# Two causal attentions in one kernel: the first pair's row maxima sent in two halves, with its first eight score blocks taken between the maxima

## The reference

```python
s1 = jnp.einsum('bhtd,bhsd->bhts', q1, k1) * scale + mask
s2 = jnp.einsum('bhtd,bhsd->bhts', q2, k2) * scale + mask
a1 = jax.nn.softmax(s1, axis=-1)
a2 = jax.nn.softmax(s2, axis=-1)
out = jnp.einsum('bhts,bhsd->bhtd', a1 - lam * a2, v)
```

## Time and profile before

| what | value |
|---|---|
| time before, median of 3 runs | 866.46 us (866.29 to 870.01) |
| the profiled execution's own time | 866.14 us |
| its span, first to last instruction | 864.4 us |
| mean granted clock of PE | 0.928 of full speed |
| first attention, first max step to last value product | about 64 to 376 us |
| second attention, likewise | about 472 to 618 us |
| busy share of PE, DVE, ACT, POOL | 88%, 61%, 50%, 50% |

### The profile page before, as it was taken

The page is one execution under the profiler, slowest core; times in us unless marked ns, Lnnn a source line. Parts: engine busy times, 40 slices in busy tenths (PEclk is TensorE's granted clock), DMA queues, the critical chain, the costliest instruction groups (busy, mean ns, idle before and its releaser), DMA issues. The chain is left out here.

```text
span 864.4 us, 12823 instructions
## 1 busy us (share of the span) xinstructions
PE 757.0 (88%) x3664; PEld 366.7 (42%) x3664; DVE 523.5 (61%) x1345; ACT 431.6 (50%) x922; POOL 430.2 (50%) x751
## 2 busy tenths in 40 slices
PE   3938999999999999954984789999569999999995
PEld 2322222223222222212752223332148888888884
DVE  3649777777777777323553877785035555555555
ACT  1431566656666655742132166776524455455552
POOL 1751556664234323421222123334277999799994
PEclk9985999999999999985997699999869999999997
DMA  5393740110020011012049362433221222122121
GB/s 183 122 295 92 160 90 15 38 47 13 20 61 18 15 45 39 20 39 67 0 148 290 88 186 68 127 98 95 66 79 48 61 61 68 51 64 71 61 64 56
DMA packets 60076, 69.84 MB, mean 81 GB/s; under 512 B 14905, under 2 KB 40858, under 8 KB 60011
## 3 DMA queue, kind: packets, MB, share of 16 engines
q1 hardware_dynamic: 60016, 69.15, 28.4%
HBM read 47.35 MB, written 15.47 MB: 73 GB/s over the span
## 5 line engine op out<-in xcount | busy, mean ns | idle before, releaser
L696 ACT ACTIVATE top<-ps 128x512 f32<-128x512 f32 (+3 forms) x384 | 171.0, 490 | 133.4 <-PE ps L643 133.3
L643 PE MATMUL ps<-mid 99*128 99x512 bf16 (+3 forms) x576 | 184.1, 335 | 8.2 <-ACT mid L696 5.0
L626 PE MATMUL ps<-mid 96*128 96x512 bf16 (+3 forms) x512 | 173.2, 360 | 15.5 <-PEq L231 11.1
L738 DVE CUSTOM_DVE_ANT_0 ps<-ps,keep 128x512 f32<-128x512 f32 (+3 forms) x320 | 161.7, 529 | 27.4 <-PE ps L626 26.8
L1479 PE MATMUL ps<-xp,wp 128*128 128x512 f32 (+1 forms) x600 | 149.3, 399 | 16.6 <-ACT wp L1531 8.7
L663 PE MATMUL ps<-top,mid 128*33 128x512 f32 (+3 forms) x768 | 161.8, 500 | 0.0
L1479 PEld LDWEIGHTS ps<-xp,wp 128*128 128x128 f32 (+1 forms) x600 | 114.6, 192 | 42.5 <-ACT xp L1533 9.1
L643 PEld LDWEIGHTS ps<-mid 99*128 99x128 bf16 x576 | 53.9, 98 | 180.8 <-ACT top L696 102.9
L820 POOL TENSOR_SCALAR_AFFINE_SELECT top<-top 128x128 f32<-128x128 f32 x256 | 71.2, 291 | 110.5 <-ACT top L696 108.1
L696 ACT ACTIVATE mid<-ps 128x512 f32<-128x512 f32 (+1 forms) x192 | 82.1, 493 | 65.1 <-PE ps L643 42.4
L742 DVE TENSOR_REDUCE top<-ps 128x1 f32<-128x512 f32 x128 | 88.2, 689 | 36.5 <-PE ps L626 35.8
(11 more groups left out here) (204 smaller groups left out, 815.5 us busy)
## 6 DMA issues: line engine op xcount, KB each, us to landing
mid<-part_scratch SPq DMA_DIRECT2D x9, 1152.0 KB, 8.8
part_scratch<-top SPq DMA_DIRECT2D x18, 384.0 KB, 5.3
top<-in_w SPq DMA_DIRECT2D x16, 396.0 KB, 3.9
cw_s<-combine_rows SPq DMA_DIRECT2D x48, 128.0 KB, 3.0
part_scratch<-top SPq DMA_DIRECT2D x18, 256.0 KB, 5.2
mid<-part_scratch SPq DMA_DIRECT2D x9, 384.0 KB, 3.9
top<-inverse_scratch SPq DMA_DIRECT2D x12, 256.0 KB
top<-in_w SPq DMA_DIRECT2D x8, 384.0 KB, 5.1
```

Source lines behind the costliest of these rows:

```text
L626: nc.tensor.matmul(ps[:, s_bank(turn), 0:w], queries(pair, m)[0:PARTS, i * P:(i + 1) * P], keys(pair, m)[0:PARTS, c * 512:c * 512 + w], st ...
L643: nc.tensor.matmul(ps[:, ST_BANK + n % AHEAD, 0:w], keys(pair, m)[0:STACK, j * P:(j + 1) * P], queries(pair, m)[0:STACK, q0:q0 + w], start ...
L696: nc.scalar.activation(pr[:, n % RING, 0:w], ps[:, ST_BANK + n % AHEAD, 0:w], ACT.Exp, scale=0.25).then_inc(p_ready, 1)
L738: ins = nc.vector.tensor_tensor_reduce(bank, bank, msk[:, 512 - w:512], -1.0 if low else 1.0, 3e38 if low else -3e38, ALU.add, ALU.min if ...
```

## The change

In both attentions the maxima of pair 0 are sent in two halves. The order on PE becomes:

1. max steps 0 to 16; after step 10 the transpose of the first half (row groups 0 to 3 of both maps, which POOL has split once step 7 is reduced);
2. scores 0, 1, 2, which wait for the first half's rows;
3. blocks 0 to 7: at each a wait for its exponential, the score three further (none from block 5 on), and one max step (17 to 24); value products 0 to 5 in pairs at blocks 3, 5 and 7;
4. max steps 25 to 35, with value products 6 and 7 and the transpose of the full maxima after step 27;
5. scores 8, 9, 10, which wait for the second half's rows; then the old loop from block 8, which at blocks 8 to 13 takes 3, 3, 3, 3, 2, 2 max steps in place of one, so that from block 14 on it is where the old one was.

DVE does its steps in the same order; its quantisation pieces of blocks 1, 3, 5 and 7 of pair 0 now follow max step 35 one behind the other. The six-bank ring ends after turn 8. The parts lie in `mt` by map, and every pair's rows go in two transfers (one a map, three rows each) where there were three (one a part); pair 0 has two for each half. ACT waits, before its first exponential, for the writes to DRAM of the stage before, since the exponentials now begin earlier over the same memory.

```diff
+                HALF, HALF_AT, FIRST, CATCH = 8, 10, 17, (3, 3, 3, 3, 2, 2)
...
+                    if n == HALF_AT:
+                        maxima_turn["half"], turns = turns, turns + 1
...
+                HALF_TURN = sum(map(alone, range(HALF)))
+                BEFORE = HALF + len(CATCH) + LEAD - sum(CATCH)
+
+                def behind(n):
+
+                    if HALF <= n < HALF + len(CATCH):
+                        done = BEFORE + sum(CATCH[0:n - HALF])
+                        return range(done, done + CATCH[n - HALF])
+                    return (n + LEAD,) if HALF <= n < BLOCKS - LEAD else ()
 
                 def s_ring(turn):
-                    return S_RING + AHEAD if turn < PAIR else S_RING
+                    return S_RING + AHEAD if turn < HALF else S_RING
...
 # TensorE
-                            if n % PAIR == 0:
-                                pe.wait_ge(landed, 48 * (pair + 1))
+                            if n == 0:
+                                pe.wait_ge(landed, 32)
+                            if n == HALF or (n % PAIR == 0 and pair > 0):
+                                pe.wait_ge(landed, 32 * (pair + 2))
...
-                        for n in range(LEAD):
+                        for n in range(FIRST):
+                            max_step(n)
+                            if n == HALF_AT:
+                                maxima("half")
+                        for n in range(AHEAD):
+                            score_step(n)
+                        for n in range(HALF):
+                            pe.wait_ge(p_ready, n + 1)
+                            if n + AHEAD < HALF:
+                                score_step(n + AHEAD)
+                            max_step(FIRST + n)
+                            if n in (3, 5, 7):
+                                value_step(n - 3)
+                                value_step(n - 2)
+                        for n in range(FIRST + HALF, BEFORE):
                             max_step(n)
                             if n == PAIR + 3:
+                                value_step(HALF - 2)
+                                value_step(HALF - 1)
                                 maxima(0)
-                        for n in range(AHEAD):
+                        for n in range(HALF, HALF + AHEAD):
                             score_step(n)
-                        for n in range(BLOCKS):
+                        for n in range(HALF, BLOCKS):
...
-                            if n + LEAD < BLOCKS:
-                                max_step(n + LEAD)
-                            if k in GROUP_AT and n > LAG:
+                            for later in behind(n):
+                                max_step(later)
+                            if k in GROUP_AT and n > HALF + LAG:
...
 # ScalarE
+                        if first:
+                            for u in range(len(UN) - SLOTS, len(UN)):
+                                act.wait_ge(*unit_written(0, u))
...
 # VectorE
-                        for n in range(LEAD):
+                        for n in range(BEFORE):
                             max_step(n)
+                            if n == HALF_AT:
+                                maxima("half")
                             if n == PAIR + 3:
                                 maxima(0)
...
-                            if n + LEAD < BLOCKS:
-                                max_step(n + LEAD)
+                            for later in behind(n):
+                                max_step(later)
...
 # GpSimd
+                            of = slice(0, NT) if half is None else slice(4 * half, 4 * half + 4)
+                            done = 3 * (pair + 1 if half != 0 else 0)
+                            if half == 0:
+                                pool.wait_ge(s_maxed, HALF_TURN)
...
-                        split(0)
+                        split(0, 0)
                         for n in range(BLOCKS):
...
+                            if n == HALF:
+                                split(0, 1)
...
 # SyncE
-                        def rows(pair):
-
-                            sp.wait_ge(s_maxed, maxima_turn[pair] + 1)
-                            for j in range(3):
-                                sp.dma_start(stack[PARTS + j:PARTS + j + 1, 2 * pair:2 * pair + 2, :]
-                                             .rearrange("o m t -> o (m t)"),
-                                             mrow[16 * j:16 * j + 16, :]).then_inc(landed, 16)
+                        def rows(pair, half=None):
+
+                            sp.wait_ge(s_maxed, maxima_turn["half" if half == 0 else pair] + 1)
+                            for m in range(2):
+                                to, at, n = stack[PARTS:STACK, 2 * pair + m, :], 24 * m, 24
+                                if half is not None:
+                                    to, at, n = to[:, 512 * half:512 * (half + 1)], 24 * half + 12 * m, 12
+                                sp.dma_start(to, mrow[at:at + n, :]).then_inc(landed, 16)
...
                         def ahead(pair):
-                            rows(pair)
+                            rows(pair, 1 if pair == 0 else None)
...
+                        rows(0, 0)
                         ahead(0)
```

More of the change, by code:

```diff
@@ L527, in attention, with part @@
                 mx = sb(f"mx{layer}", [P, 2, 4, 2], F32, here)
[L528 removed]
+                mr = sb(f"mr{layer}", [P, 2, NT], F32, here)
                 mt = sb(f"mt{layer}", [P, P], BF16, here)
[L530 removed]
+                zero = sb(f"zero{layer}", [P, 2, NT], F32, here)
                 mrow = sb(f"mrow{layer}", [48, P], BF16, here)
[L533 to L534 removed]
+                def part(j, half):
+                    if half is None:
+                        return mt[:, 0:48].rearrange("p (m j i) -> p m j i", m=2, j=3)[:, :, j, :]
+                    return mt[:, 24 * half:24 * half + 24].rearrange("p (m j i) -> p m j i", m=2, j=3)[:, :, j, :]
                 if first:
@@ L632, in maxima @@
                             turn = maxima_turn[pair]
-                            pe.wait_ge(mt_ready, pair + 1)
-                            pe.wait_ge(s_maxed, turn - S_RING + 1)
+                            if pair == "half":
+                                pe.wait_ge(mt_ready, 1)
+                            else:
+                                pe.wait_ge(mt_ready, pair + 2)
+                            pe.wait_ge(s_maxed, turn - s_ring(turn) + 1)
                             nc.tensor.transpose(psb[:, s_bank(turn), 0:P], mt[:, :], idb[:, :]).then_inc(s_ready, 1)
@@ L725, in max_step @@
                             if k == 0 and pair >= 2:
-                                dve.wait_ge(mt_ready, pair - 1)
+                                dve.wait_ge(mt_ready, pair)
                             dve.wait_ge(s_ready, turn + 1)
@@ L751, in maxima @@
                             dve.wait_ge(s_ready, turn + 1)
-                            if pair > 0:
-                                dve.wait_ge(landed, 48 * pair)
+                            if pair == 0:
+                                dve.wait_ge(landed, 32)
+                            elif pair != "half":
+                                dve.wait_ge(landed, 32 * (pair + 1))
                             nc.vector.tensor_copy(mrow[:, :], psb[0:48, s_bank(turn), 0:P]).then_inc(s_maxed, 1)
@@ L798, in _ @@
                         nc.gpsimd.memset(mt[:, :], 0.0).then_inc(cleared, 1)
-                        nc.gpsimd.memset(zero[:, :], 0.0).then_inc(cleared, 1)
+                        nc.gpsimd.memset(zero[:, :, :], 0.0).then_inc(cleared, 1)
                         pool.wait_ge(cleared, 2)
[L802 to L813, removed]
-                            nc.gpsimd.tensor_tensor(part(2), mr[:, 0, :], part(1), ALU.subtract).then_inc(mt_ready, 1)
@@ new lines, in split @@
+                        def split(pair, half=None):
+                            of = slice(0, NT) if half is None else slice(4 * half, 4 * half + 4)
+                            done = 3 * (pair + 1 if half != 0 else 0)
+                            if half == 0:
+                                pool.wait_ge(s_maxed, HALF_TURN)
+                            else:
+                                pool.wait_ge(nm_ready, pair + 1)
+                                pool.wait_ge(s_ready, maxima_turn[pair - 1 if pair > 0 else "half"] + 1)
+                            a, rest, nil = nm[:, pair % 2, :, of], mr[:, :, of], zero[:, :, of]
+                            to = [part(j, half) for j in range(3)]
+                            nc.gpsimd.tensor_tensor(to[0], a, nil, ALU.add).then_inc(pch, 1)
+                            pool.wait_ge(pch, done + 1)
+                            nc.gpsimd.tensor_tensor(rest, a, to[0], ALU.subtract).then_inc(pch, 1)
+                            pool.wait_ge(pch, done + 2)
+                            nc.gpsimd.tensor_tensor(to[1], rest, nil, ALU.add).then_inc(pch, 1)
```

(3 more changed lines are left out.)

4 lines of the change are left out of this document (2 added, 2 removed).

## The result

The changed kernel takes 869.47 us (median of 20 runs, 867.5 to 873.7) against 867.69 for the kernel before in 20 runs beside it; the ratio is 1.0028, 95% interval 1.0014 to 1.0041, which is 2.4 us slower (1.2 to 3.6). The forecast was 866.4, no change against the median of 866.46 it started from, with a range of 863.0 to 870.0: the time lies in the range, but a slowdown clear of noise was not forecast. The kernel before has 1.2 us more in these 20 runs than in the three behind the forecast, so the ratio says more than the two absolute times. Its profiled execution took 869.56 us with a span of 867.6, against 866.14 and 864.4.

The account below looks back on a forecast made before the run. A chain of DVE reductions bounds the fronts, PE the loop after them. 866.14 + 0.5 + 0.7 + 0.4 - 1.6 = 866.1 us (fronts, low clock, rows), plus a third for the median: forecast 866.4, range 863.0 to 870.0.

Parts of the forecast that it names:

- the accounting of VectorE's waits in the fronts: Both attentions' fronts (first max step to the shared point): waits put into DVE make them 0.5 and 0.7 us later.
- the shared point: Transpose of pair 1's maxima at block 13, where both orders meet; forecast 96.4 and 502.5 us, before 95.89 and 501.82.
- Half transfer and first score: First attention's front: half rows land at 72.6 us, score 0 starts at about 72.8, against 82.58.
- Blocks 0 to 7: First front: DVE idle 2.0 us ahead of step 17 and 1.35 ahead of step 21; copy ends at 82.8.
- Part a: First max step to transpose of pair 0's full maxima: forecast 17.9 and 17.8 us, against 13.58 and 13.70 before.
- rival of a low clock: Clock stays at 1.2 GHz through both fronts: +3 to +4 us a front, 872 to 873; chance 0.17.
- Low clock after block 7: Blocks 8 and on may start at 1.2 GHz; DVE's pace hides most: 0.2 us a front, ends 0 and 0.9.
- part b: From transpose of pair 0's full maxima to pair 1's: forecast 14.2 and 13.0 us, against 18.03 and 16.44 before.
- Quantisation in one row: First front, between max steps 35 and 36: four pieces together add 1.3 us to DVE's chain, formerly in idle time.
- Row transfers: Two a pair save one 0.59 us issue where PE waits for rows: 0.6 + 0.6 + 0.4 = 1.6 sooner.
- PE's pace as a gain: Rival: PE, not DVE, sets the pace after score 8; 861.2 us in all, half of it 864; chance 0.12.
- The middles: Both attentions past their fronts, where PE bounds the loop: unchanged to 0.5 us.

Follow-up runs that it names:

- e3: Changed kernel with one unused product of 512 columns after each of max steps 25 to 35, both attentions: 869.91 us, ratio 1.0034.
- e9: Changed kernel with two max steps at blocks 0 and 1, and unused products after max steps in both stretches of max steps alone: 866.08 us, ratio 0.9984.
- e10: e9 with an unused product also after each max step of blocks 8, 9 and 10: 866.5 us, ratio 0.9994.
- e11: e10 with the quantisation's five pieces moved one pair later (pairs 1 to 5): 869.98 us in one run.
- e1: Kernel before, old order of blocks, with only the two row transfers a pair by map and ACT's added wait: 866.28 us against 867.25, ratio 0.9983.
- e4: Kernel before with one unused product of 512 columns after each of max steps 8 to 37, both attentions: 865.96 us, ratio 1.000.
- e5: Changed kernel with an unused product after each of max steps 8 to 16 and 25 to 35, both attentions: 865.57 us, ratio 0.9991.
- e8: Changed kernel with two max steps in place of one at blocks 0 and 1, no unused products: 867.26 us, ratio 0.9993.
- e12: The changed kernel run once more, nothing altered, to see how its front moves between executions: 869.6 us.

## Why the prediction missed the sign

The step that failed is the accounting of VectorE's waits in the fronts, 0.5 and 0.7 us later in the sum; in the two profiles of the changed kernel they are 3.0 and 2.0 later in the first attention, 2.7 and 2.0 in the second. The prediction named this itself as the reading if the shared point came more than 2 us off: it came 2.2 off in the first attention (98.56 for 96.4) and 3.5 in the second (505.99 for 502.5), 2.1 without the later start. Term by term:

- **Half transfer and first score: right.** 72.62 us against 72.8; the queue was empty and nothing landed late.
- **Blocks 0 to 7: right in kind, short in size.** The two waits forecast were there, with 3.97 us in all for 3.35. The sum took over the old order's clock, at 1.2 GHz for value products 0 and 1 and at full speed from products 2 and 3 on. But PE was at 1.2 GHz for most of these too (1.22 us where the old order had 0.84), and step 23 waits again (0.60). Part a is 19.12 and 19.31 where the sum had 17.9; in the second attention 19.41 and 18.23 for 17.8. That is the larger term of the error, 0.4 to 1.6 us a front. The prediction had it among the ends ("phase of the clock in blocks 0 to 7 (-0.9 to +2)") and put it at nothing in the sum. The sign that it gave for its rival of a low clock, "if the clock is still low at products 2 and 3, about 79 us", is what the trace shows (0.50 in the window of 78 to 80).
- **Low clock after block 7: mis-sized in the first attention.** "DVE's pace hides most of it" held only at full clock: there part b is 13.9 (e3, e9, e10), near the sum's 14.2. At 1.2 GHz PE paces the end of blocks 8 to 13, as the wait of 1.23 after the fold shows: 15.45 and 14.26. I took 0.2; it cost 0.3 to 1.5 in the first attention and some 0.2 to 0.6 in the second. The rival of the low clock "in part (low only in the catch-up)" gave 868 to 869, 1.5 to 2.5 above the median that the forecast started from; the measured 2.4 lies in that.
- **Quantisation in one row: wrong.** 1.3 us were added to VectorE's chain; e11 shows that they mostly fill the wait for exponential 8, which the sum had counted in the second attention (0.6) and left out of the first.
- **Row transfers: open.** The sum had 0.59 saved at each of three waits, 1.6. An issue by map takes 0.756, so 0.3 is saved and not 0.59. The waits fell by more than that in e1, from 1.8 to 1.2 in the first attention and from 1.0 to none in the second, 1.6 in all, so the total agrees with the forecast, though not for its reason; but ACT's wait grew by as much (2.1 to 3.7). e1's interval, 3.3 sooner to 0.3 later, holds both 1.6 and nothing.
- **PE's pace as a gain: refuted.** It asked for step 28 before 80.5 us; it began at 83.54 in the changed kernel. Even with full clock and earlier steps (e10) the fronts are 0.4 us below before's, while the old order with the same products (e4) has 29.79 in the first.
- **The middles.** They were to stay within 0.5 us; the first attention's was 1.0 shorter in the profile. Eight of the twelve experiments have it 0.8 to 1.7 shorter than before's and the others within 0.6 of it, so one profile of before is too little to say why.

That the time still fell into the range is owed to the range's width and not to the sum.

So the new order loses because it gives VectorE's time away for PE's, in a stretch that VectorE paces: its max steps wait behind scores and value products, which are up to twice as long at 1.2 GHz. Shown: with PE at full clock in blocks 0 to 7 (e5) or with VectorE given work over the long products (e8), the time is no longer measurably above before's, and with full clock after block 7 alone (e3) it still is. The two are largely one loss, since both together (e9) give little more. Not tested by itself: the six-bank ring ending at turn 8.

Open: whether the shorter fronts of e4 and e10 reach the total. The executions of the kernel before alone spread over 8 us (863.66 to 871.66), and the intervals of 10 to 12 runs reach 1.2 us and more to either side. Open too: ACT's wait for output transfers in the second attention, 2.7 to 3.9 us in all kernels but the one before (2.1), with three row transfers (e4, 3.2) or two; what delays them was not tried.

## What to carry to other kernels

Before moving work of an idle engine forward, ask what stands between two instructions of the engine that paces the stretch, and price that at the clock which the row of this stretch shows, not at the loop's. Where the clock may be at either level, work out the sum at both instead of carrying over the moment of its rise from another order of work: here the rise came 2 us later after score 0, and that was the larger term of the error. Measure one front over several executions before a microsecond of it is believed.

## What the runs showed of the hardware

- At 1.2 GHz value products of 512 columns took 1.92 us a pair where they took 1.05 at 2.4. An unused product after each max step kept PE at 1.00 where it fell to 0.50 without (e3, windows of 88 to 94 us). It did not always last: in e5, with the same products, the clock was at 0.56 in the window of 90 to 92, in the blocks behind them, and in e10, where the products went on through blocks 8 to 10, it stayed at 1.00.
- A stretch in which the profile shows PE busy throughout can stay at 1.2 GHz: in the changed kernel 2.00 of 2.00 us at 0.50 (window of 78 to 80).
- The same program's clock came back by 94 us in one execution and after 96 in another (e12 and the changed kernel), and the part between moved by 1.2 us.
- A transfer of 24 partitions of 256 bytes to three partitions takes 0.756 us to issue on SyncE, one of 16 partitions to a single one 0.589.
